# Moving the output-projection products of the first batch's units from the ends of heads two and four to other heads, in a fused decoder-layer kernel

## The chip, the cores and the metric

The kernel runs on one core of one Trainium2 chip. The metric is the device time of one execution in microseconds (us). TensorE is called PE here, VectorE DVE, ScalarE ACT, GpSimd POOL, and SyncE, which issues the DMAs, SP.

## The reference, cut to what matters

```python
x = layernorm(x + attn(x, Wq, Wk, Wv, Wo))          # x: 4 x 512 x 512, 32 query heads, 8 key/value heads
x = layernorm(x + smooth_quant_mlp(x, fside, ctx))  # int8-style MLP, per-batch weights
x = layernorm(x + ffn(x, sign(up), sign(down)))     # 512 -> 2048 -> 512, relu

def attn(x):
    q, k, v = x @ Wq.T, x @ Wk.T, x @ Wv.T          # head width 64, rope on q and k
    p = softmax(causal(q @ k.T / 8))                # 4 query heads share one k/v head
    return (p @ v) @ Wo.T                           # the last product: "output products" below
```

## The kernel before, in words

**Units and heads.** Attention is cut into 32 units. A step g (0 to 15) is one key/value head for two of the four batches; within it b = 0 and b = 1 are the two batches, and unit u = 2g + b. Steps 0 to 7 do batches 0 and 1, steps 8 to 15 batches 2 and 3. A unit has four query heads, h = 0 to 3; the text calls them first to fourth head. In steps 8 to 15 (`half == 1`) single instructions of the quantized MLP of finished batches are slotted in by a written-out schedule (`later(...)`), and after attention the feed-forward part runs.

**One head.** Each engine has a program order of its own, and the engines meet only at semaphores. On PE a head is: transpose blocks 0 and 1 of its probabilities into `ps_t` (L1897), the first two score tiles of the head after it (L1852, into `ps_s`), a *middle* place where one output product may stand, transpose block 2, the last two score tiles, an *end* place for other work, and `values` (L1909, eight matmuls into `ps_o`). DVE meanwhile takes the low parts `pT_lo` (L1562), adds the two halves of the head's result (L1499), makes the row maxima of the next head's scores (`softmax_max`, L1491, four per head), then does the additions to `y` and the reciprocals of the row sums (L1582). ACT exponentiates the next head's four tiles (L1268) and copies the high parts `pT_hi` (L1276). The transposes of a head wait for all four exponentials of that head.

**The end places of a unit.** First head: product "odd" of the next queries (12 matmuls) and `recips` (four transposes, L1919). Second: "vT" (four small transposes, L1865), whose result ACT and DVE take (`low_v`, L1481). Third: "kv" (12 matmuls) and `recips`. Fourth: "even" (12 matmuls).

**Output products.** A unit's result is multiplied by Wo in four products (one per 128 rows), `project_out`, six matmuls each (L1852, `m<-woT_hi,o_hi` and so on). Each is written into the one PSUM tile `m1`, and DVE adds it to `y` in `add_y` (L1514). The `recips` transposes use `m1` too; `normalize` (L1505) reads those. So seven writers of `m1` in a unit of b = 0 and five in one of b = 1 follow one another, in the order of the list `M1_ORDER`; each waits until DVE has read the one before:

```python
def project_out(idx, u, buf, i):
    pe.wait_ge(m1_read, idx - 1)
```

A unit of b = 0 has five products: "out3" of the unit two back (first head, middle), then "out0", "out1", "out2" of the unit before it (second, third and fourth head, middle) and "out3 early" (fourth head, end, behind "even"). A unit of b = 1 has three: "out0" at the end of the second head behind "vT", "out1" and "out2" in the middles of the third and fourth. The unit g = 0, b = 0 has none; so 15 units of b = 0 have five each. In step 15 there is no "kv" and no "even", and in its b = 0 unit four transposes of `y` (L2013) stand ahead of the second, third and fourth of the heads' first transposes; they wait for `low_v` and then for DVE's `lo` parts (L1783). `o_lo` (L1094, on POOL) is what "out0" waits for besides `m1`.

Of the kernel before, what the change touches and what calls it, by code (L numbers as in the profile page):

```python
# [496 lines left out]
def build(nc, x, x_t, wq_t, wkv_t, wo_t, fside, fside_t, ctx, ctx_t, ffn_t, up_s, down_s, out_s, cos_t, sin_t, sin_k_t, out):  # L497
    with ExitStack() as es:
# [186 lines left out]
        def wait(eng, s, v):  # L685

            if not isinstance(v, int) or v > 0:
# [7 lines left out]
        M0_ORDER = [["odd", "vT", "kv", "even"]] * HALF  # L695


        M1_ORDER = [["out3", "recip1", "out0", "out1", "recip0", "out2", "out3 early"],
                    ["recip1", "out0", "out1", "recip0", "out2"]]

        def place(order, b, what):
# [5 lines left out]
        def m1_fill(g, b, what):  # L707
# [3 lines left out]

            return g * sum(len(w) for w in M1_ORDER) + (place(M1_ORDER, b, what) - (len(M1_ORDER[0]) - 1))

# [6 lines left out]
        def before(g, b):  # L720

            return (g, b - 1) if b > 0 else (g - 1, HALF - 1)

        U = STEPS * HALF

# [738 lines left out]
        def _(dve):  # L1464
# [14 lines left out]
            def low_v(u, buf):  # L1479
                dve.wait_ge(v_hi, (u + 1) * 2)  # L1480
                dve.tensor_tensor(v_st[:, buf, :, HD:2 * HD], m0[:, 0:KT * HD].rearrange("p (k d) -> p k d", k=KT),  # L1481
                                  f32(v_st[:, buf, :, 0:HD]), ALU.subtract).then_inc(m0_read, 1)
# [24 lines left out]
            def add_y(g, b, half, what):  # L1507

                to = batch(g, b, half, 2 if what == "out3" else 1)
                if b == 1 and (is_step(g, 0) or is_step(g, HKV)):  # L1510
                    dve.wait_ge(x_in[to], 16 if to == 0 else 32)
                dve.wait_ge(m1_full, m1_fill(g, b, what))
                t = to * QT + int(what[3])
                dve.tensor_tensor(y[:, t, :], y[:, t, :], m1[:, :], ALU.add).then_inc(m1_read, 1)  # L1514
# [32 lines left out]
            def body(g, half):  # L1547
                first = is_step(g, 0)
                last = is_step(g, STEPS - 1)
                for b in range(HALF):  # L1550
                    u = g * HALF + b
                    nxt = not (last and b == HALF - 1)
                    nxt2 = not last
                    prev = not (first and b == 0)
                    for h in range(G):
                        n = u * G + h
                        more = nxt or h < G - 1
                        for k in range(3):
                            dve.wait_ge(p_hi, n * 3 + (k + 1))
                            w = len(T_BLOCKS[k])  # L1560
                            d = slice(PT_FIRST[k], PT_FIRST[k] + w)
                            dve.tensor_tensor(pT_lo[:, d, :], ps_t[:, (h + k) % 2, 0:P * w].rearrange("p (w c) -> p w c", c=P),  # L1562
                                              f32(pT_hi[:, d, :]), ALU.subtract).then_inc(p_lo, 1)
                            if k == 0 and more:
                                softmax_max(n + 1, (h + 1) % 2, 0)
                                softmax_max(n + 1, (h + 1) % 2, 1)
                            if k == 0 and (prev or h > 0):
                                add_o(n - 1, (h - 1) % G, u * 2 + (h - 1) // 2)
                        if more:
                            softmax_max(n + 1, (h + 1) % 2, 2)  # L1570
                            softmax_max(n + 1, (h + 1) % 2, 3)
                        if (is_step(g, 0) or is_step(g, HKV)) and (b, h) == (HALF - 1, G - 1):
                            dve.wait_ge(x_in[half * HALF + HALF - 1], 32)
                        if h == 0 and b != 1 and prev:
                            add_y(g, b, half, "out3")
                        if h > 0 and prev:
                            add_y(g, b, half, f"out{h - 1}")

                        dve.wait_ge(exped, n * 4 + 4)
                        if h % 2 == 0:  # L1580
                            wait(dve, r_repd, u * 2 + h // 2)
                        dve.reciprocal(r_inv[:, :, h // 2, h % 2], row_sum[:, h % 2, :]).then_inc(r_done, 1)  # L1582
                        if half == 1:
                            later("dve1", slot(g, b, h))
                        if h == 0:
                            if prev:
                                normalize(*before(g, b), 1)
                            if nxt:
                                rope_q(m0_fill(g, b, "odd"), u + 1, "odd")
                        if h == 1 and nxt:  # L1590
                            low_v(u + 1, (b + 1) % 2)
                        if h == 2:
                            normalize(g, b, 0)
                        if h == 3:
                            if nxt2:
                                rope_q(m0_fill(g, b, "even"), u + 2, "even")
                            if b == 0 and prev:
                                add_y(g, b, half, "out3 early")
                        if half == 1:
                            later("dve2", slot(g, b, h))  # L1600

# [246 lines left out]
        def _(pe):  # L1848
# [102 lines left out]
            def body(g, half):  # L1951
                first = is_step(g, 0)
                last = is_step(g, STEPS - 1)
                for b in range(HALF):
                    u = g * HALF + b
                    nxt = not (last and b == HALF - 1)
                    nxt2 = not last
                    prev = not (first and b == 0)
                    for h in range(G):
                        n = u * G + h  # L1960
                        more = nxt or h < G - 1
                        ahead = (n + 1, u, h + 1, b % 2) if h < G - 1 else (n + 1, u + 1, 0, (b + 1) % 2)
                        if half == 1:
                            later("pe1", slot(g, b, h))
                        transpose_probs(n, h, 0)
                        transpose_probs(n, h, 1)
                        if more:
                            scores(*ahead, 0)
                            scores(*ahead, 1)
                        if h == 0 and b != 1 and prev:  # L1970
                            project_out(m1_fill(g, b, "out3"), u - 2, b % 2, 3)
                        if h > 0 and prev and (b, h) != (1, 1):
                            project_out(m1_fill(g, b, f"out{h - 1}"), u - 1, (b + 1) % 2, h - 1)
                        if half == 1:
                            later("pe2", slot(g, b, h))
                        transpose_probs(n, h, 2)
                        if more:
                            scores(*ahead, 2)
                            scores(*ahead, 3)
                        if h == 0:  # L1980
                            if nxt:
                                project(m0_fill(g, b, "odd"), (b + 1) % HALF, "odd")
                            if prev:
                                recips(*before(g, b), 1)
                        if h == 1 and nxt:
                            project(m0_fill(g, b, "vT"), (b + 1) % HALF, "vT")
                        if (b, h) == (1, 1):

                            pe.wait_ge(w_lo, w_count(g, "o1"))
                            project_out(m1_fill(g, b, "out0"), u - 1, 0, 0)  # L1990
                        if h == 2:
                            if nxt2:
                                if is_step(g, HKV - 1):
                                    pe.wait_ge(x_lo, KT * (HALF + b + 1))
                                if b == 0:
                                    pe.wait_ge(w_lo, w_count(g + 1, "kv"))
                                project(m0_fill(g, b, "kv"), b, "kv")
                            recips(g, b, 0)
                        if h == 3:
                            if nxt2:  # L2000
                                if b == 0:
                                    pe.wait_ge(w_lo, w_count(g + 1, "q1"))
                                project(m0_fill(g, b, "even"), b, "even")
                            if b == 0 and prev:
                                project_out(m1_fill(g, b, "out3 early"), u - 1, (b + 1) % 2, 3)
                        if half == 1:
                            later("pe3", slot(g, b, h))
                        values(n, h, b % 2)
# [207 lines left out]
```

## Time and profile before

| what | value |
|---|---|
| median of 3 runs | 1388.5 us (1386.83 to 1388.78) |
| the profiled execution: its own time | 1389.54 us |
| its span, first to last instruction | 1387.5 us |
| mean granted TensorE clock | 0.984 of full speed |
| PE matmul busy | 1294.3 us (93% of the span) |
| DVE, ACT, POOL busy | 1012.8, 904.9, 784.7 us (73%, 65%, 57%) |
| attention | up to about 1106 us |

A row of the timeline is: start in us from the span's start, duration, engine, line, operation, output<-inputs, sizes and count; in brackets the idle time of the engine ahead of it and what ended that. Matmuls are pipelined: one of 128x512 is shown with about 0.4 us, but the next starts 0.23 us after it. So PE's cost is read from start to start.

### The profile page before, as it was taken

The numbers are of one execution on the slowest core, as the hardware profiler recorded it, in microseconds if no ns is written. First come the engines' busy times: TensorE is split into PE (matmuls) and PEld (weight loads), VectorE is DVE, ScalarE is ACT, GpSimd is POOL, SyncE is SP. The second block draws the span as 40 slices with busy tenths as digits, with TensorE's granted clock in tenths as the row PEclk, the third lists the DMA queues.
The fourth block names the chain that finished last, engine by engine and source line by source line (L and its number), as shares of the span: only waits on it lengthen the run. The fifth ranks groups of instructions, "written<-read, shape, count | busy, mean of one in ns | idle before, by whom it ended". The sixth has DMA issues, their size and how long they took to land.

```text
span 1387.5 us, 25190 instructions
## 1 busy us (share of the span) xinstructions
PE 1294.3 (93%) x7112; PEld 1075.5 (78%) x7112; DVE 1012.8 (73%) x2492; ACT 904.9 (65%) x2140; POOL 784.7 (57%) x685
## 2 busy tenths in 40 slices
PE   5899999999999999989999999999998899999996
PEld 3788878888888877878877787888776676778784
DVE  3677777777677777898987888778896798875422
ACT  3676777777766776766775776677766756565332
POOL 4555565655556575646873557486661264746553
PEclk8999999999999999999999999999999999999998
DMA  4722222222222223233222222222223602100000
GB/s 138 234 62 54 61 58 63 61 69 62 73 67 54 61 55 92 85 91 85 69 69 54 69 69 55 85 54 69 58 59 121 240 15 71 56 16 31 1 31 30
DMA packets 55285, 98.78 MB, mean 71 GB/s; under 512 B 11792, under 2 KB 13840, under 8 KB 54288
## 3 DMA queue, kind: packets, MB, share of 16 engines
q1 hardware_dynamic: 55184, 97.57, 25.3%
q8 instruction: 47, 0.77, 0.2%
q14 instruction: 54, 0.44, 0.1%
HBM read 51.39 MB, written 4.19 MB: 40 GB/s over the span
## 4 chain that ended last, share of the span: by engine, by line
PE 75%; DVE 10%; ACT 6%; issue 5%; POOL 2%; SPq 0%; DMA 0%; ACTq 0%; DVEq 0%; POOLq 0%
PE m L1852 30%; PE ps_s L1852 9%; PE ps_o L1909 9%; PE ps_t L1897 7%; PE m L2144 7%; PE ps_t L2160 3%; PE ps_s L2160 3%; DVE pT_lo L1562 2%; PE m L1919 2%; ACT pT_hi L1276 2%; DVE o_sum L1505 1%; ACT probs L1268 1%; DVE probs L1491 1%; POOL o_lo L1094 1%; PE pc L2013 1%
## 5 line engine op out<-in xcount | busy, mean ns | idle before, releaser
L1268 ACT ACTIVATE probs<-probs,neg_max 128x128 f32<-128x128 f32 (+3 forms) x512 | 285.3, 559 | 155.7 <-DVE neg_max L1491 155.1
L1562 DVE TENSOR_TENSOR pT_lo<-ps_t,pT_hi 128x512 fp32r<-128x512 f32 (+1 forms) x384 | 220.9, 595 | 141.2 <-ACT pT_hi L1276 138.8
L1491 DVE CUSTOM_DVE_ANT_0 probs<-ps_s,mask 128x128 f32<-128x128 f32 (+3 forms) x512 | 228.3, 482 | 9.4 <-PE ps_s L1852 9.3
L1852 PE MATMUL ps_s<-k_st,q_st 128*128 128x256 f32 (+2 forms) x1024 | 231.7, 348 | 2.4 <-DMA q_st<-q_tmp 2.0
L1897 PE MATMUL ps_t<-ident,probs 128*128 128x128 f32 x1280 | 185.6, 276 | 45.5 <-DVE pT_lo L1562 35.4
L1897 PEld LDWEIGHTS ps_t<-ident,probs 128*128 128x128 f32 x1280 | 147.5, 141 | 70.3 <-DVE pT_lo L1562 44.7
L1276 ACT ACTIVATE pT_hi<-ps_t 128x512 fp32r<-128x512 f32 (+1 forms) x384 | 186.3, 519 | 13.9 <-PE ps_t L1897 10.9
L1094 POOL TENSOR_TENSOR o_lo<-o_sum,o_hi 128x512 fp32r<-128x512 f32 x64 | 81.9, 1279 | 194.1 <-ACT o_hi L1290 194.0
L1909 PE MATMUL ps_o<-pT_hi,v_st 128*128 128x256 f32 (+2 forms) x512 | 169.5, 342 | 0.0
L1909 PE MATMUL ps_o<-pT_lo,v_st 128*128 128x256 f32 (+2 forms) x512 | 156.6, 327 | 0.0
L1852 PEld LDWEIGHTS ps_s<-k_st,q_st 128*128 128x128 f32 x1024 | 151.8, 191 | 5.5 <-issue 2.6
L1144 POOL TENSOR_TENSOR hid_lo<-hid,hid_hi 128x512 fp32r<-128x512 f32 x64 | 84.2, 1315 | 124.4 <-ACT hid_hi L1455 124.4
L1283 ACT ACTIVATE o_part<-ps_o 64x512 f32<-64x512 f32 x128 | 75.9, 593 | 90.6 <-PE ps_o L1909 87.8
L1453 ACT ACTIVATE hid<-m,up_col 128x512 f32<-128x512 f32 x64 | 44.0, 688 | 112.1 <-PE m L2144 109.8
L1852 PE MATMUL m<-woT_hi,o_hi 128*128 128x512 f32 x256 | 105.3, 411 | 6.6 <-POOL o_lo L1094 4.6
L1852 PE MATMUL m<-xT_hi,wqT_hi 128*128 128x512 f32 x256 | 102.6, 401 | 2.8 <-DVEq L1477 2.0
L1909 PEld LDWEIGHTS ps_o<-pT_hi,v_st 128*128 128x128 f32 x512 | 97.8, 191 | 9.4 <-DVE pT_lo L1562 0.5
L1909 PEld LDWEIGHTS ps_o<-pT_lo,v_st 128*128 128x128 f32 x512 | 98.1, 192 | 7.7
L1852 PE MATMUL m<-xT_lo,wqT_hi 128*128 128x512 f32 x256 | 102.8, 402 | 0.0
L1852 PE MATMUL m<-xT_hi,wqT_lo 128*128 128x512 f32 x256 | 102.3, 399 | 0.0
L1852 PE MATMUL m<-woT_lo,o_hi 128*128 128x512 f32 x256 | 101.6, 397 | 0.0
L1852 PE MATMUL m<-woT_hi,o_lo 128*128 128x512 f32 x256 | 101.6, 397 | 0.0
(259 smaller groups left out, 3069.4 us busy)
## 6 DMA issues: line engine op xcount, KB each, us to landing
q_st<-q_tmp SPq DMA_DIRECT2D x512, 64.0 KB, 2.0
raw<-in_wq_t SPq DMA_DIRECT2D x32, 256.0 KB, 3.0
k_st<-k_st SPq DMA_DIRECT2D x64, 128.0 KB, 2.3
raw<-in_wo_t SPq DMA_DIRECT2D x32, 256.0 KB, 3.0
raw_b<-in_ffn_t SPq DMA_DIRECT2D x10, 512.0 KB, 7.5
raw<-in_wkv_t SPq DMA_DIRECT2D x16, 256.0 KB, 3.6
y<-in_x SPq DMA_DIRECT2D x4, 1024.0 KB, 6.8
w_gu<-in_fside_t SPq DMA_DIRECT2D x4, 1024.0 KB, 7.1
```

The costliest lines, as they stand in the source:

```text
L1094: pool.tensor_tensor(o_lo[:, buf, p, :], o_sum[:, :], f32(o_hi[:, buf, p, :]), ALU.subtract).then_inc(o_los, 1)
L1144: pool.tensor_tensor(hid_lo[:, n % 2, :], hid[:, n % 2, :], f32(hid_hi[:, n % 2, :]), ALU.subtract).then_inc(hid_los, 1)
L1268: act.activation(probs[:, h % 2, SO[i]:SO[i] + SW[i]], probs[:, h % 2, SO[i]:SO[i] + SW[i]], ACT.Exp, bias=neg_max[:, h % 2, i:i + 1], sca ...
L1276: act.activation(pT_hi[:, PT_FIRST[k]:PT_FIRST[k] + w, :], ps_t[:, (h + k) % 2, 0:P * w].rearrange("p (w c) -> p w c", c=P), ACT.Copy).the ...
L1283: act.activation(o_part[a:a + HD, :], ps_o[c:c + HD, :], ACT.Copy).then_inc(o_copied, 1)
L1491: dve.tensor_tensor_reduce(out=probs[:, h % 2, SO[i]:SO[i] + SW[i]], in0=ps_s[:, i % 2, 0:SW[i]], in1=mask[:, L - SW[i]:L], scale=-SCALE, ...
L1562: dve.tensor_tensor(pT_lo[:, d, :], ps_t[:, (h + k) % 2, 0:P * w].rearrange("p (w c) -> p w c", c=P), f32(pT_hi[:, d, :]), ALU.subtract).t ...
L1852: i = pe.matmul(dst, a, c, start=(j == 0), stop=(j == len(terms) - 1))
L1897: i = pe.transpose(ps_t[:, (h + k) % 2, P * c:P * (c + 1)], probs[:, h % 2, at:at + P], ident[:, :])
L1909: i = pe.matmul(ps_o[:, q0:L], v_st[:, buf, kt, v0:v0 + P], pT[:, blocks, :], start=(j == 0 and s == 0), stop=(j == 3 and s == 1))
L2144: i = pe.matmul(m0[:, :], w[:, P * k:P * (k + 1)], x2[:, b % 2, k, :], start=(k == 0 and x2 is xT_hi), stop=(k == KT - 1 and x2 is xT_lo))
L2160: i = pe.matmul(down_bank(t), hd[:, m % 2, P * t:P * (t + 1)], w[:, D:2 * D], start=(h == 0 and hd is hid_hi), stop=(h == HT - 1 and hd is ...
```

## The change

In the units of b = 0, "out1" moves from the middle of the third head to the end of the second (behind "vT"), "out2" from the middle of the fourth to the middle of the third, "out3 early" from the end of the fourth to its middle. The writer order of `m1` and the place of DVE's additions go with them: the addition of "out1" now stands behind `low_v` in the second head. Nothing is added or dropped, and units of b = 1 stay as they are.

```diff
-        M1_ORDER = [["out3", "recip1", "out0", "out1", "recip0", "out2", "out3 early"],
+        M1_ORDER = [["out3", "recip1", "out0", "out1", "out2", "recip0", "out3 early"],
                     ["recip1", "out0", "out1", "recip0", "out2"]]
...
+        def out_at(b, h):
+            return ["out0", "out2", "out3 early"][h - 1] if b == 0 else f"out{h - 1}"
...
@@ DVE's order
                         if h > 0 and prev:
-                            add_y(g, b, half, f"out{h - 1}")
+                            add_y(g, b, half, out_at(b, h))
...
                         if h == 1 and nxt:
                             low_v(u + 1, (b + 1) % 2)
+                        if (b, h) == (0, 1) and prev:
+                            add_y(g, b, half, "out1")
...
                                 rope_q(m0_fill(g, b, "even"), u + 2, "even")
-                            if b == 0 and prev:
-                                add_y(g, b, half, "out3 early")
...
@@ PE's order
                         if h > 0 and prev and (b, h) != (1, 1):
-                            project_out(m1_fill(g, b, f"out{h - 1}"), u - 1, (b + 1) % 2, h - 1)
+                            project_out(m1_fill(g, b, out_at(b, h)), u - 1, (b + 1) % 2, int(out_at(b, h)[3]))
...
                             project(m0_fill(g, b, "vT"), (b + 1) % HALF, "vT")
+                        if (b, h) == (0, 1) and prev:
+                            project_out(m1_fill(g, b, "out1"), u - 1, 1, 1)
...
                                 project(m0_fill(g, b, "even"), b, "even")
-                            if b == 0 and prev:
-                                project_out(m1_fill(g, b, "out3 early"), u - 1, (b + 1) % 2, 3)
```

## Rows read from the trace of the kernel before

**Rows 1.** The page: busy time of each engine, then the chain that ended last.
```profile
PE 1294.3 (93%) x7112; PEld 1075.5 (78%) x7112; DVE 1012.8 (73%) x2492; ACT 904.9 (65%) x2140; POOL 784.7 (57%) x685
...
PE 75%; DVE 10%; ACT 6%; issue 5%; POOL 2%; SPq 0%; DMA 0%; ACTq 0%; DVEq 0%; POOLq 0%
```

**Rows 2.** Waits of PE from 80 to 1048 us: total, times, longest.
```profile
PE ps_t L1897 <- DVE pT_lo L1562: 29.8, 31, 3.7
PE ps_t L1897 <- ACT probs L1268: 8.8, 16, 1.3
```

**Rows 3.** Timeline, all engines, second head of the b = 0 unit of step 6.
```profile
431.87 0.46 PE L1865 MATMUL m<-ident,k_tmp 64*128 64x64 f32 x4
432.25 0.50 PE L1909 MATMUL ps_o<-pT_hi,v_st 128*128 128x512 f32 x1
...
433.13 0.68 DVE L1514 TENSOR_TENSOR y<-y,m 128x512 f32<-128x512 f32 x1
...
433.88 0.19 ACT L1268 ACTIVATION_READ_ACCUMULATOR probs<-probs,neg_max 128x1 f32 x1
...
434.21 1.06 PE L1897 MATMUL ps_t<-ident,probs 128*128 128x128 f32 x8 [0.40 <-ACT probs L1268]
```

**Rows 4.** Timeline of PE, same unit: "out0", then the fourth head's end.
```profile
429.27 0.47 PE L1852 MATMUL m<-woT_hi,o_hi 128*128 128x512 f32 x1 [0.24 <-POOL o_lo L1094]
...
430.74 0.38 PE L1897 MATMUL ps_t<-ident,probs 128*128 128x128 f32 x2
...
449.18 0.39 PE L1852 MATMUL m<-woT_hi,o_hi 128*128 128x512 f32 x1
...
450.54 0.39 PE L1909 MATMUL ps_o<-pT_hi,v_st 128*128 128x512 f32 x1
...
451.81 1.03 PE L1897 MATMUL ps_t<-ident,probs 128*128 128x128 f32 x8
```

**Rows 5.** Timeline, second head in steps 5 and 7, b = 0.
```profile
369.81 0.68 DVE L1514 TENSOR_TENSOR y<-y,m 128x512 f32<-128x512 f32 x1
...
370.79 1.09 PE L1897 MATMUL ps_t<-ident,probs 128*128 128x128 f32 x8 [0.40 <-ACT probs L1268]
...
496.43 0.68 DVE L1514 TENSOR_TENSOR y<-y,m 128x512 f32<-128x512 f32 x1
...
498.43 1.06 PE L1897 MATMUL ps_t<-ident,probs 128*128 128x128 f32 x8 [1.21 <-ACT probs L1268]
```

**Rows 6.** Timeline, b = 0 unit of step 15: second head, then fourth head's end.
```profile
1037.62 0.67 DVE L1514 TENSOR_TENSOR y<-y,m 128x512 f32<-128x512 f32 x1
...
1040.18 0.63 PE L2013 MATMUL m<-ident,y 128*128 128x128 f32 x4 [2.12 <-DVE v_st L1481]
1040.64 1.04 PE L1897 MATMUL ps_t<-ident,probs 128*128 128x128 f32 x8
...
1054.12 0.67 DVE L1514 TENSOR_TENSOR y<-y,m 128x512 f32<-128x512 f32 x1
...
1054.81 0.65 DVE L1783 TENSOR_TENSOR xT_lo<-m,xT_hi 128x512 fp32r<-128x512 f32 x1
1054.85 0.50 PE L1852 MATMUL m<-woT_hi,o_hi 128*128 128x512 f32 x1 [1.85 <-DVE y L1514]
...
1059.64 1.04 PE L1897 MATMUL ps_t<-ident,probs 128*128 128x128 f32 x8
```

**Rows 7.** Timeline of PE: two more waits of about two microseconds.
```profile
1046.84 0.66 PE L1919 MATMUL m<-ident,r_rep 128*128 128x128 f32 x4 [1.81 <-DVE y L1514]
...
1079.49 0.66 PE L1919 MATMUL m<-ident,r_rep 128*128 128x128 f32 x4 [2.39 <-DVE y L1514]
```

**Rows 8.** Stretches behind such waits; the column after the five engines is the granted clock.
```profile
1056.10:1059.60 3.50, 3.50 (x14) 3.20 (x13) 0.69 (x1) 0.57 (x1) 0.00 (x0) 0.52 0.97 394
1079.90:1083.30 3.40, 3.40 (x17) 3.21 (x16) 0.89 (x2) 1.23 (x2) 1.27 (x1) 0.53 1.03 419
1047.00:1050.00 3.00, 3.00 (x25) 2.91 (x25) 1.14 (x2) 1.55 (x4) 1.03 (x1) 1.00 0.60 146
```

## The prediction, made before the changed kernel was run

> **What bounds the kernel.** I read the page first: PE is busy for 93% of the span, and the chain that ended last lies on PE for three quarters of it [rows 1]. So within attention the question is what makes PE idle, not how much another engine has to do. The table of PE's waits then shows two main kinds [rows 2]: transposes that wait for `pT_lo`, and transposes at the start of a head that wait for the exponentials, 16 times and 8.8 us in all. Last I read the timeline of single units. The second head of every b = 0 unit has the shortest end place, "vT" alone, and there the third head's transposes start 0.40 us late, since the last exponential's sum ends at 434.07 [rows 3]. The fourth head has the longest end: "even" and a product, 449.18 to 450.54 [rows 4]. PE's matmuls are the same before and after; the change pays only through waits that go or come.
>
> **Fourth head.** "out3 early" leaves its end. From its first matmul to the first of `values` is 450.54 - 449.18 = 1.36 us [rows 4], all of it on PE's path: -1.36. `values` then ends 1.36 earlier, at about 450.45. The next transposes can start there if the exponentials are ready. The addition of "out2" does not stand in the way, for the product now in the middle of the fourth head takes exactly the place and the size of the one that was there. The same holds for "out2" in the middle of the third. These two trades cost nothing; what covers their reads of `m1` is the same as before ("kv" with `recips`, and the transposes and scores).
>
> **Second head, the new wait.** "out1" stands behind "vT" and ahead of `values`. As every writer of `m1` it waits for the read of the one before, here DVE's addition of "out0". DVE does that only after the fourth row maximum of the next head, and that follows PE's last score tile directly ahead of "vT". So DVE is late by construction: the addition starts at 433.13 and ends at 433.81 [rows 3], while PE is through with "vT" and would go on at 432.25. How long the hand-over takes is seen in step 15, where the same situation exists already (a product with nothing but scores between it and the product before): the addition ends at 1054.12 + 0.67 = 1054.79, the matmul starts at 1054.85 [rows 6], 0.06 us later. So "out1" starts at 433.87, 1.62 us after the point where PE would have gone on. A product that starts from a standing PE takes 430.74 - 429.27 = 1.47 us [rows 4], `values` takes 451.81 - 450.54 = 1.27 [rows 4], and the third head's transposes start at 433.87 + 1.47 + 1.27 = 436.61 instead of 434.21: +2.40. The old 0.40 us wait for the exponentials is in this sum, since they are long done. Net for the unit: 2.40 - 1.36 = +1.04 us.
>
> **What is queued behind the wait.** On PE: "out1", `values`, the next transposes, in order; ACT's copy of `ps_o` waits for `values`. On DVE the new addition stands behind `low_v` and ahead of the scheduled MLP work and the third head's `pT_lo`, but that needs transposes which PE does after "out1" and `values`, 2.7 us later; the 0.6 us of the addition are hidden there. "out2", one head on, needs that addition read: "out1" ends at about 435.3 and its addition at 436.0, while "out2" can start no sooner than 1.4 us of transposes and scores behind 436.6. SP's and POOL's queues get nothing new.
>
> **The other units.** By the same arithmetic on their own rows: in step 5 the addition ends at 370.49, the transposes would start at 370.49 + 0.06 + 2.74 = 373.29 against 370.79 [rows 5], +2.50, net +1.14. Steps 1 to 4 repeat this to within 0.01; steps 8 to 14 repeat step 6 to within 0.01. In step 7 ACT has extra work and PE waited 1.21 us already; there it is 497.11 + 2.80 = 499.91 against 498.43 [rows 5], +1.48, net +0.12. Sum over steps 1 to 14: 5 x 1.14 + 8 x 1.04 + 0.12 = +14.1.
>
> **Step 15** differs. In the second head PE waited 2.12 us for `low_v` before four transposes [rows 6]. Now "out1" starts at 1038.29 + 0.06 = 1038.35, `values` ends at 1041.09, the four transposes take 0.46 (1040.18 to 1040.64), and the head starts at 1041.55 instead of 1040.64: +0.9. In the fourth head the standing wait of 1.85 us, "out3 early" and a slow `values` behind it go away. PE will wait instead for the low part that ends at 1054.81 + 0.65 = 1055.46, then do 0.46 of transposes: 1056.0 against 1059.64 [rows 6], -3.6. Net -2.7. All units together: +11.4 us.
>
> **The granted clock.** The waits here are long enough to ask whether the clock drops from its 2.4 GHz level to the 1.2 GHz one. After PE stood for 1.85 and for 2.39 us [rows 6, 7] the clock fell for about 3.4 us (0.52 and 0.53 [rows 8]); after 2.12 us and 1.81 us [rows 6, 7] the rows go on at full pace, and the stretch behind the second shows 1.00 [rows 8]. So two of the four waits of this size cost a fall. The new waits are 1.6 us long, 14 of them (that of step 15 apart), a little shorter than all four: I take one in three, between four and five falls. A fall costs 3.5 x (1 - 0.52) = 1.7 us where PE sets the pace. That is +7.5 us; the bounds are no fall (0) and two in three (+16). The Trainium skill, "TensorE: Matmul & The Clock Gate", section "Why this matters for your kernels", advises to avoid PE-idle gaps between bursts of matmuls, and the gap that it names is longer than all four waits here. By that page the clock would stay up and the sum would be +11.4; this trace's fall after 1.85 us speaks against it.
>
> **Sum.** The profiled execution took 1389.54 us, 1.04 above the median of the runs (1388.5), and 2.04 more than its span; I count the difference of +11.4 + 7.5 = +18.9 from the median: 1407.4 us.
>
> **Rivals.**
>
> *A: the wait, with the clock up.* 1388.5 + 11.4 = 1399.9. For it: every new wait is shorter than the shortest one that was followed by a fall. One fall would still belong here. Chance 0.30.
>
> *B: the clock falls in most of the units.* 1388.5 + 11.4 + 16 = 1415.9. For it: "vT" and the transposes beside the wait are small work, and half of the comparable waits cost a fall. Chance 0.15.
>
> *C, on the other side: the addition of "out0" is not late.* If DVE were done with it by the time "vT" is, "out1" would follow without a wait: third head at 432.25 + 1.37 + 1.27 = 434.89, +0.68, net -0.68 a unit; 14 of them -9.5, with step 15's fourth head -3.6, about 1375.5. It decides at a wait of about 0.7 us, above which a unit loses. Against it: the fourth row maximum alone ends after 433.1 [rows 3], and it can't start before the scores that precede "vT". Chance 0.05.
>
> *D: the added time is taken out of later waits.* The 29.8 us of waits for `pT_lo` [rows 2] would have to shrink by what the second heads add. They hang on ACT's and DVE's order behind `values`, which moves along with PE; only single ones, where DVE's MLP work is late in the third head, can be absorbed. If it happened in steps 8 to 14: about 1388.5 + 5.7 + 1.0 + 0.1 - 2.7 = 1392.6 or, with some large waits gone, no change. Chance 0.08 (half of it within 0.2% of before or faster).
>
> **The numbers.** My forecast, the wait and some falls of the clock (2 to 7), has the remaining 0.42: 1407.4, its own range 1402 to 1412. The 8-in-10 range reaches down to just below A and up to B: 1397 to 1417. About 0.2% (2.8 us) is what a measurement of this kernel can tell from no change. Slower by more: forecast, A, B and half of D, 0.91; same 0.03; faster 0.06.
>
> **What would show it.** In the new profile, a wait of about 1.5 us ahead of a `m<-woT_hi,o_hi` matmul, released by DVE's `y` at L1514's successor, in all 15 b = 0 units, right behind "vT"; no wait for exponentials at their third heads; the fourth head's end 1.36 us shorter; in step 15 the 1.85 us wait gone; stretches of clock near 0.5 behind some of the new waits, and the mean clock below 0.984. I am wrong if DVE's addition is found ahead of "vT"'s end, if the waits for `pT_lo` shrink by as much, or if the clock does something else.

## The result, and the profile of the changed kernel

The changed kernel takes 1398.9 us (median of 5 runs, 1395.3 to 1401.1), the kernel before 1388.5 us (5 runs, 1386.8 to 1390.7): a ratio of 1.0074, 95% interval 1.0062 to 1.0086. That is 10.4 us slower, against 18.9 forecast; the time lies in the wide range of the prediction (1397 to 1417), and below the forecast's own 1402 to 1412. The profiled execution took 1398.74 us with a span of 1397.0 us.

First the page of the changed kernel; its row that begins with PE's busy time answers to the first of [rows 1], its last row to the second. Most lines of the program now have numbers higher by five (L1514 is L1519).

```profile
span 1397.0 us, 25180 instructions
...
PE 1290.2 (92%) x7112; PEld 1074.9 (77%) x7112; DVE 1010.5 (72%) x2492; ACT 905.9 (65%) x2140; POOL 784.9 (56%) x685
...
PE 71%; DVE 12%; issue 7%; ACT 5%; POOL 4%; SPq 0%; DMA 0%; DVEq 0%; POOLq 0%; ACTq 0%
```

PE has the same work and a lower share; DVE's share of the chain went up, from 10% to 12%, PE's went down, from 75% to 71%. Next PE's waits, from 80 to 1058 us:

```profile
PE ps_t L1902 <- DVE pT_lo L1567: 28.2, 30, 3.6
PE m L1857 <- DVE y L1519: 24.1, 15, 1.9
...
PE ps_t L1902 <- ACT probs L1273: 1.7, 2, 1.3
```

A kind of wait is new: an output product for DVE's addition to `y`, 15 times, 24.1 us. The waits for the exponentials went from 16 and 8.8 us to 2 and 1.7 us, those for `pT_lo` hardly moved (29.8 before [rows 2]). Now the timeline of the second head in step 6, all engines, which answers to [rows 3]:

```profile
435.32 0.46 PE L1870 MATMUL m<-ident,k_tmp 64*128 64x64 f32 x4
...
436.61 0.68 DVE L1519 TENSOR_TENSOR y<-y,m 128x512 f32<-128x512 f32 x1
...
437.34 0.50 PE L1857 MATMUL m<-woT_hi,o_hi 128*128 128x512 f32 x1 [1.56 <-DVE y L1519]
...
438.84 0.39 PE L1914 MATMUL ps_o<-pT_hi,v_st 128*128 128x512 f32 x1
...
440.12 1.03 PE L1902 MATMUL ps_t<-ident,probs 128*128 128x128 f32 x8
```

From "vT" to the next head's transposes it is now 4.80 us, before 2.34: +2.46, where 2.40 was forecast. The addition ends at 437.29, the matmul starts 0.05 us later.

The starts of `values` in the 128 heads, changed kernel minus kernel before, give the whole account. Taken is the second of its eight matmuls, since the first is drawn out by 0.1 us where it stands right behind "vT". Each number below is that shift in us at the first to the fourth head of a unit:

```
step 1  b=0    -2.06   1.06   0.42  -0.94        step 9  b=0     5.30   9.07   9.28   7.93
step 2  b=0    -0.95   2.15   1.49   0.14        step 10 b=0     8.16  11.03  10.18   8.84
step 5  b=0     2.36   5.46   4.81   3.45        step 12 b=0    10.11  13.13  11.63  10.28
step 6  b=0     3.47   6.48   5.85   4.50        step 12 b=1    10.39   6.36   6.79   6.78
step 6  b=1     4.52   4.51   4.52   4.52        step 13 b=0     6.78  11.56  10.70   9.33
step 7  b=0     4.52   7.41   5.55   4.23        step 15 b=0    11.87  15.48  14.35  10.54
step 8  b=0     4.24   7.24   6.62   5.29        step 15 b=1    10.76  10.79  10.69   9.63
```

How to read it: within a unit the shift jumps up in the second head, gives back 0.65 in the third and 1.35 in the fourth; in a unit of b = 1 it stands still. Steps 1 to 5 add 1.10 us each, steps 6 and 8 about 1.05, step 7 takes 0.29 off. From the first head of step 1 to the last of step 15 the changed kernel loses 11.7 us. It had come 2.06 us early to step 1: that is in the lead-in, which the change doesn't touch, and where the clock was granted differently (0.94 over the first 80 us, 0.91 before). The last experiment below keeps the old order and shows 0.94 there too, so the change isn't what makes it.

### The profile page after: what moved, and what is told of

It reads as the page before. It is cut to its first block, busy times and chain, and to the rows that moved or that the text cites. A ratio compares the mean times of both kernels' runs of the same rounds, so it can differ in the third digit from the quotient of the medians.

```text
span 1397.0 us, 25180 instructions
## 1 busy us (share of the span) xinstructions
PE 1290.2 (92%) x7112; PEld 1074.9 (77%) x7112; DVE 1010.5 (72%) x2492; ACT 905.9 (65%) x2140; POOL 784.9 (56%) x685
## 4 chain that ended last, share of the span: by engine, by line
PE 71%; DVE 12%; issue 7%; ACT 5%; POOL 4%; SPq 0%; DMA 0%; DVEq 0%; POOLq 0%; ACTq 0%
PE m L1857 28%; PE ps_s L1857 9%; PE ps_o L1914 9%; PE m L2149 7%; PE ps_t L1902 7%; PE ps_t L2165 3%; PE ps_s L2165 3%; DVE pT_lo L1567 2%; PE m L1924 2%; DVE probs L1496 2%; ACT pT_hi L1281 2%; POOL o_lo L1099 1%; DVE o_sum L1510 1%; DVE y L1519 1%; ACT o_hi L1295 1%
## 5 line engine op out<-in xcount | busy, mean ns | idle before, releaser
L1857 PE MATMUL m<-woT_hi,o_hi 128*128 128x512 f32 x256 | 107.3, 419 | 28.9 <-DVE y L1519 24.1
```

Of the source, the lines that this page charges most:

```text
L1857: i = pe.matmul(dst, a, c, start=(j == 0), stop=(j == len(terms) - 1))
```

## The experiments

All are the changed kernel with the edit shown, except where the text says otherwise. Times are medians; the kernel before took 1387.9 to 1388.7 us beside them.

### The addition of "out0" earlier in DVE's order

```diff
                             if k == 0 and (prev or h > 0):
                                 add_o(n - 1, (h - 1) % G, u * 2 + (h - 1) // 2)
+                            if k == 1 and (b, h) == (0, 1) and prev:
+                                add_y(g, b, half, "out0")
...
-                        if h > 0 and prev:
+                        if h > 0 and prev and (b, h) != (0, 1):
                             add_y(g, b, half, out_at(b, h))
```

> The changed kernel, with DVE's addition of out0 in the second head of b = 0 placed ahead of the third pT_lo instead of behind the four row maxima. Theory (the late addition is the whole loss): out1 follows vT without a wait, each unit gains 0.7 us on the kernel before and step 15 some 3.6 us, so about 1375.5 us, against 1398.9 for the changed kernel and 1388.5 before. The addition pushes the maxima and exponentials 0.4 to 0.6 us later, to about 434.6 in the unit of step 6, still ahead of the 434.9 at which PE comes to the transposes. Rival (the second head gets too full whatever the order, since DVE and ACT are pushed back too): 1390 to 1399 us, with a wait for pT_lo or the exponentials in place of the one for y.

Measured: 1370.9 us, ratio to before 0.9874 (0.9858 to 0.9891). The theory holds, and the version beats both kernels, by 17 and by 28 us. It lies 4.6 us below the expected 1375.5: steps 1 to 6 gain 0.6 us each on the kernel before, as rival C of the prediction had it (0.68), and most of the rest is a gain of 4 us in step 12 that is told further down. Its timeline in step 6, all engines:

```profile
425.82 0.67 DVE L1519 TENSOR_TENSOR y<-y,m 128x512 f32<-128x512 f32 x1
...
426.29 0.46 PE L1872 MATMUL m<-ident,k_tmp 64*128 64x64 f32 x4
...
426.68 0.50 PE L1859 MATMUL m<-woT_hi,o_hi 128*128 128x512 f32 x1
...
428.57 0.19 ACT L1273 ACTIVATION_READ_ACCUMULATOR probs<-probs,neg_max 128x1 f32 x1
...
429.45 1.03 PE L1904 MATMUL ps_t<-ident,probs 128*128 128x128 f32 x8
```

The addition is over at 426.49, and "out1" follows "vT" with no idle time. From "vT" to the transposes it is 3.16 us. The exponentials are done at 428.76, before PE comes to them.

### The same addition a little later

The edit is the same with `k == 2` in place of `k == 1`.

> As the one before, but the addition of out0 behind the third pT_lo and ahead of the last two row maxima, 0.6 us later. Theory: out1 waits about 0.55 to 0.65 us for it; a unit comes out 0.0 to 0.1 us better than before and step 15 gains 3.6 us, so 1383 to 1385 us. Rival (a wait of this length is covered by something else): 1376, as with no wait; rival (second head too full): 1390 to 1399.

Measured: 1381.1 us, ratio 0.9947 (0.9931 to 0.9964), 2 us below the expected range. PE's waits for `y` are 8.4 us in all, 16 times.

### The addition later still

```diff
                         if (b, h) == (0, 1) and prev:
+                            add_y(g, b, half, "out0")
                             add_y(g, b, half, "out1")
```

(with the `!= (0, 1)` line of the first experiment)

> The changed kernel with the addition of out0 made still later, behind low_v. Theory: out1 starts about 1.9 us later than in the changed kernel (wait of 3.5 us instead of 1.6), 15 times, +28 us: 1427 us, if the clock falls no more often than before. If each wait of 3.5 us is followed by a fall of the granted clock that costs 1.7 us and nothing else goes away: another 20 to 25 us, about 1450. Rival (the wait is not what PE's time hangs on): 1399.

Measured: 1449.8 us, ratio 1.0441 (1.0424 to 1.0459). PE's waits for `y`, and the stretches of 84 to 500 and 500 to 1100 us, whose clock stands after the five engines:

```profile
PE m L1858 <- DVE y L1519: 53.9, 15, 4.7
...
84.00:500.00 416.00, 384.06 (x2159) 328.74 (x2158) 281.65 (x771) 276.63 (x718) 218.97 (x188) 0.98 0.24 59
500.00:1100.00 600.00, 543.43 (x3060) 460.62 (x3058) 465.94 (x1199) 396.48 (x1005) 355.05 (x311) 0.96 0.25 66
```

The waits grew by 29.8 us, the time by 50.9. The rest goes with the clock: in the changed kernel the same two stretches show 1.00 and 0.98. Each of the 15 waits (3.3 to 4.7 us) has a fall of the clock with it, which begins during the wait or up to 1.3 us behind it. That of step 2, where the wait ends at 184.29:

```profile
184.50:187.90 3.40, 3.40 (x9) 2.63 (x9) 0.69 (x1) 0.00 (x0) 1.18 (x2) 0.50 0.44 101
```

That is the case for which 1450 us was expected. So the price of a wait has two parts, its own length and, where it is long, a slower TensorE behind it.

The time rises with the wait over the four places of one addition. Waits of PE for `y` in an `m<-woT_hi,o_hi` matmul against the time:

| addition of "out0" | waits, us | time, us |
|---|---|---|
| behind the second `pT_lo` | 0.8 | 1370.9 |
| behind the third `pT_lo` | 8.4 | 1381.1 |
| behind the maxima (the changed kernel) | 24.1 | 1398.9 |
| behind `low_v` | 53.9 | 1449.8 |

### "out1" behind `values`

```diff
-                        if (b, h) == (0, 1) and prev:
-                            project_out(m1_fill(g, b, "out1"), u - 1, 1, 1)
...
                         values(n, h, b % 2)
+                        if (b, h) == (0, 1) and prev:
+                            project_out(m1_fill(g, b, "out1"), u - 1, 1, 1)
```

> The changed kernel with out1 behind the second head's values on PE instead of ahead of them; DVE's order as in the changed kernel. Theory: 1.27 of the 1.62 us of the wait is covered by values; the third head's transposes start 1.1 us later than before the change, the fourth head gains 1.36, so a unit gains 0.2 us and step 15 about 3.6: about 1381.5 us. Rival (the product's own 1.47 us behind vT is what costs, wherever it stands in the second head's end): about 1398.

Measured: 1378.7 us, ratio 0.9931 (0.9915 to 0.9948). DVE's order is that of the changed kernel and the product is still in the second head; only PE has something to do while DVE finishes. The waits for `y` are 2.3 us in all, and the time is 2.8 us below the expected 1381.5. So the product's own 1.47 us were never the loss.

### The wait filled with matmuls of no use

```diff
                         if (b, h) == (0, 1) and prev:
+                            wait(pe, o_added, n)
+                            for j in range(6):
+                                pe.matmul(ps_o[:, :], o_hi[:, 1, 0, 0:P], woT_hi[:, 0, :], start=True, stop=True)
                             project_out(m1_fill(g, b, "out1"), u - 1, 1, 1)
```

> The changed kernel with six matmuls of no use on PE ahead of out1 in the second heads of b = 0, written into the ps_o tile that values overwrites; they take 1.4 of the 1.6 us for which PE stands there. Nothing else changes, so without a part of the clock the time is that of the changed kernel, 1399. If the low-clock stretches behind four of the new waits cost what I had counted (1.6 to 1.7 us each) and nothing takes their place: 1392. If falls of the clock come elsewhere instead: 1398 to 1400.

Measured: 1391.7 us (10 runs, 1390.4 to 1397.1), ratio 1.0034 (1.0017 to 1.0051), close to the 1392 expected if the new falls go. The median is 7.2 us below the changed kernel's, the ratios (1.0034 and 1.0074) put the difference at 5.6 us, with six matmuls more in each of 15 units. The slowest of the 10 runs had a lower mean clock than the profiled one (0.987 against 0.991). Its timeline of PE in step 6:

```profile
434.31 0.46 PE L1870 MATMUL m<-ident,k_tmp 64*128 64x64 f32 x4
434.70 1.65 PE L1995 MATMUL ps_o<-woT_hi,o_hi 128*128 128x512 f32 x6
436.33 0.50 PE L1857 MATMUL m<-woT_hi,o_hi 128*128 128x512 f32 x1
...
439.11 1.03 PE L1902 MATMUL ps_t<-ident,probs 128*128 128x128 f32 x8
```

"vT" to transposes is 4.80 us, as in the changed kernel. In steps 1 to 8 the two kernels keep their distance to 0.15 us. They part in steps 9, 13, 14 and 15, by 1.56, 1.50, 1.57 and 1.56 us, and by 1.1 in step 10. In the changed kernel the four second heads of those steps are followed by a slow stretch:

```profile
637.80:641.20 3.40, 3.40 (x11) 2.78 (x12) 2.07 (x3) 0.56 (x3) 3.40 (x5) 0.60 0.50 113
914.80:918.20 3.40, 3.09 (x7) 2.48 (x8) 0.90 (x4) 1.54 (x5) 3.40 (x5) 0.52 0.46 104
983.00:986.40 3.40, 3.40 (x10) 2.67 (x10) 1.82 (x4) 0.49 (x2) 3.40 (x4) 0.53 0.48 110
1050.60:1054.00 3.40, 3.40 (x13) 2.94 (x12) 1.97 (x3) 1.27 (x3) 1.42 (x2) 0.63 0.43 97
437.50:440.50 3.00, 3.00 (x18) 2.65 (x19) 1.11 (x2) 0.76 (x4) 3.00 (x4) 1.00 0.48 109
```

The last line is the one of step 6, where the clock stayed up behind a wait of 1.56 us; the first stands behind one of 1.55. So the same wait can cost 1.6 us more or nothing. With PE kept busy these four falls are gone, 6.2 us in the profiled executions. The 1.1 us of step 10 are not one of them: there a fall of 6.8 us behind a wait of 3.2 us for `pT_lo`, which the kernel before has too, came out half as long.

### "out3 early" at the fourth head's end again

```diff
-                        if h > 0 and prev and (b, h) != (1, 1):
+                        if h > 0 and prev and (b, h) not in ((1, 1), (0, 3)):
                             project_out(m1_fill(g, b, out_at(b, h)), u - 1, (b + 1) % 2, int(out_at(b, h)[3]))
...
                                 project(m0_fill(g, b, "even"), b, "even")
+                            if b == 0 and prev:
+                                project_out(m1_fill(g, b, "out3 early"), u - 1, 1, 3)
```

(and DVE's addition of it behind `rope_q` again)

> The changed kernel with out3 early at the end of the fourth head again, behind even, and so with nothing in the fourth head's middle. My step says that a product's place within the fourth head is free of charge. Against it stands the pattern of heads with an empty middle, where PE waits 0.7 us for pT_lo: then 15 times 0.7 us, about 1409 us. If the places are equal: 1399.

Measured: 1418.2 us, ratio 1.0213 (1.0177 to 1.0249), 19 us more than the changed kernel, where I had 10 for the wait. PE's waits for `pT_lo` over 80 to 1150 us rose from 32 times and 29.8 us in the changed kernel to:

```profile
PE ps_t L1904 <- DVE pT_lo L1567: 42.6, 46, 3.7
```

Fourteen waits more; those of the fourth heads in steps 1 to 7 are 0.75 to 0.85 us long. Such a fourth head costs 1.0 us more in all, 0.2 above its wait. Of the rest 2.4 us are in the b = 1 unit of step 12 (below), 2 us stood already before step 1 (the clock of the first 80 us is 0.91 here), and the clock fell more often (0.982 against 0.985 as the mean). So here a place in the middle is worth more than one at the end.

### The change in step 15 alone

The kernel before, with the new order and places where `g == STEPS - 1` and the old ones elsewhere:

```diff
-            return g * sum(len(w) for w in M1_ORDER) + (place(M1_ORDER, b, what) - (len(M1_ORDER[0]) - 1))
+            order = M1_ORDER if isinstance(g, int) and g == STEPS - 1 else M1_OLD
+            return g * sum(len(w) for w in order) + (place(order, b, what) - (len(order[0]) - 1))
```

> The kernel before, with the change made in step 15 alone (one unit of b = 0). Theory: the second head loses 0.9 us to the wait for the addition, the fourth gains 3.6 because its standing wait of 1.85 us and the product leave its end; with a fall of the clock behind the new wait, as in the changed kernel, 1.7 of it go again. So 1 to 2.7 us faster than before: 1386 to 1387.5 us. Rival (the loss of 10 us comes from step 15 or from what follows it): slower than before.

Measured: 1386.0 us, ratio 0.9989 (0.9980 to 0.9998). It gains 1 to 2 us, as expected; the interval only just leaves out no change. The new wait, 1.77 us, has a fall of the clock behind it here too.

### The early addition in the old order

The kernel before, with nothing but the first experiment's edit of DVE's order.

> The kernel before, in its old order, with nothing but DVE's addition of out0 in the second head of b = 0 moved ahead of the third pT_lo. Theory (the early addition is good only because out1 follows): nothing waits for it in the old order, and it pushes the row maxima and so the exponentials back by 0.4 us, for which PE already waited 0.40 us in the third head; 14 times 0.4 us, about 1394 us. Rival (the early addition itself is what makes the version with 1370.9 us fast): well under 1388, down to 1375.

Measured: 1391.1 us, ratio 1.0022 (1.0013 to 1.0032). The early addition by itself costs 3 us, where 6 had been expected. PE's wait in the third head of step 6 is longer than the 0.40 us of [rows 3]:

```profile
434.43 1.06 PE L1899 MATMUL ps_t<-ident,probs 128*128 128x128 f32 x8 [0.67 <-ACT probs L1268]
```

So neither half is good alone: the products' new places cost 10 us, the early addition 3 us, and both together save 17.

## Why the prediction was right, and where it was off

**The wait in the second head** was right in mechanism, place, number and size: 15 waits, 24.1 us, of 1.42 to 1.90 us each; forecast were 14 of 1.6 us, and one in step 15 to which the prediction gave no length of its own. The four places of the addition, and the version with the wait covered by `values`, show that it is the cause. Taking it away turns +10.4 us into -17.

**The unit's sum.** Forecast +1.14 in steps 1 to 5 and +1.04 in steps 6 and 8; measured 1.10 and 1.05. Step 7 was to be +0.12 and is -0.29. Step 10 comes to +0.7 and step 12 to +0.3 in its b = 0 unit, both forecast at 1.04. Part of the added time is taken out of a later wait in step 12: the kernel before waited 0.49 us for `pT_lo` at 840.5, in the third head, and the changed one doesn't.

```profile
840.52 0.44 PE L1897 MATMUL ps_t<-ident,probs 128*128 128x128 f32 x2 [0.49 <-DVE pT_lo L1562]
```

That is rival D on a small scale. In steps 7 and 10 it is not shown what takes the 0.4 us each. Steps 9, 11, 13 and 14 add 1.3, 1.3, 1.1 and 0.9 us once the falls of the clock behind their new waits are taken off. Steps 1 to 14 so come to +12.9, forecast +14.1. I had named rival D and given it no share of the sum.

**The fourth head** gave back 1.35 us, forecast 1.36. That the *middle* place costs nothing held because both kernels fill it. Emptied, it costs 1.0 us a head, and the same empty middles stand in the first two heads of every b = 1 unit of both kernels.

**Step 15** was forecast at -2.7 without a fall of the clock and so about -1.0 with one; its b = 0 unit went from +11.87 to +10.76, -1.1, with the fall of 1050.6 us in it. The parts fit as well: +2.5 up to the third head (0.9 and the fall), then -3.6. PE's wait for the low part, at 1069.94, was 1.31 us:

```profile
1069.94 0.63 PE L2018 MATMUL m<-ident,y 128*128 128x128 f32 x4 [1.31 <-DVE xT_lo L1788]
```

**The granted clock** is the step that failed: "between four and five falls ... +7.5 us". The falls behind the new waits were there, four of them, and the filled version puts them at 6.2 us. What I left out is that falls of the kernel before would go, other than the one inside the -3.6 of step 15. The stretch of 500 to 1100 us shows 0.98 in both kernels:

```profile
500.00:1100.00 600.00, 552.55 (x3187) 468.49 (x3187) 484.59 (x1244) 416.30 (x1046) 348.41 (x306) 0.98 0.28 76
```

In attention the kernel before has falls at 595, 729, 868, 1056 and 1080 us, the changed one at 601, 638, 737, 915, 983 and 1051 us; each lasts 3.4 us, those at 729, 868 and 737 us twice that. Three of the old ones are missing in the changed kernel. That behind the 1.85 us wait of step 15 goes with its cause, and it is in the -3.6 that I had counted. That behind the 2.39 us wait [rows 7] is gone although the wait is still there; the last head of step 15 comes 1.1 us less late for it. And the double one of step 12 goes where the wait ahead of it gets shorter, next; that unit of b = 1 gains 3.6 us in all, 1.5 of them the shorter wait, which leaves 2.1 for the clock. So both kernels spend the same time at the low clock, seven times 3.4 us. Counted as the forecast counts, with the fall of 1056 us inside the -3.6, the clock's share is 6.2 - 1.1 - 2.1 = 3.0 us, not 7.5.

**The whole difference** between the profiled executions, +9.5 us against +18.9, is then: 4.5 us less for the clock, 1.5 less for the shorter wait of step 12, 1.3 less in the sum of steps 1 to 14, and 2.1 in the lead-in. The first is the term that the prediction mis-sized, the second nothing in it foresaw, and the last has nothing to do with the change. That the time comes to rival A's 1399.9 is luck: A had said that the clock would not fall behind the new waits, and it fell four times.

**A gain that nothing of mine foresaw** is step 12, b = 1: -4.0 us at its second head. DVE's rows there, in the kernel before:

```profile
864.77 3.27 DVE L1615 TENSOR_TENSOR sm_b<-sm_b,bounds 128x4 f32<-128x4 f32 x1
868.07 0.16 DVE L1616 TENSOR_TENSOR sm_b<-sm_b,bounds 128x4 f32<-128x4 f32 x1
```

and in the changed kernel:

```profile
875.15 0.76 DVE L1620 TENSOR_TENSOR sm_b<-sm_b,bounds 128x4 f32<-128x4 f32 x1
875.94 1.19 DVE L1621 TENSOR_TENSOR sm_b<-sm_b,bounds 128x4 f32<-128x4 f32 x1
```

The two small operations end 1.5 us sooner against what is around them, PE's wait for the `pT_lo` behind them falls from 3.71 to 2.23 us, and the clock, which had fallen for 6.8 us there, stays up. The first row is the kernel before, the second the changed one:

```profile
868.50:875.30 6.80, 6.23 (x18) 4.77 (x19) 4.21 (x13) 5.24 (x15) 2.52 (x2) 0.50 0.22 50
878.00:884.80 6.80, 6.80 (x41) 5.80 (x42) 5.93 (x20) 6.55 (x18) 3.99 (x6) 1.00 0.26 60
```

The same -4.0 appears in the version with the early addition, and it is lost again (+3.0 against the changed kernel) where "out3 early" stands at the fourth head's end. In all ten versions it goes with that edit: the six with "out3 early" in the fourth head's middle show a wait of 2.2 us here, the four with it at the end one of 3.7. Why DVE's start shifts by 0.07 us against POOL's row with it, I did not test.

**What stays open.** Whether a wait of 1.5 to 2.4 us is followed by a fall can't be told from its length alone, and the runs here don't settle what decides. So some us of the difference between any two of these kernels hang on it; the runs of the changed kernel themselves spread over 5.8 us.

## What to carry to other kernels

A move of a product on PE is also a move of its reader: before putting a second writer of one buffer into a stage, look at where in the other engine's program order the read of the first stands, not at how busy that engine is. Here one line in DVE's order turned a loss of 10 us into a gain of 17, and either edit alone lost. And when a change adds waits of some microseconds to TensorE, count the clock's falls on both sides, those that come and those of the old kernel that may go.

## What the runs showed of the hardware

**A wait of 1.5 us can be enough for a fall of the clock, and length alone doesn't decide it.** Behind waits of 1.55 and 1.90 us the clock fell to about half (0.60 and 0.52 above), behind one of 1.56 it stayed at 1.00. Useless matmuls in the gap were worth 5.6 to 7.2 us. The Trainium skill, "TensorE: Matmul & The Clock Gate", section "Why this matters for your kernels", advises against idle gaps longer than all of these; by it none of these falls should have come, and the measurement decides.

**A tiny DVE operation beside a row of POOL operations can take as long as several of them.** The 128x4 operation at 864.77, of a kind that takes 0.16 us (the next one, at 868.07), took 3.27 us while POOL ran without a pause. POOL's rows of that stretch, kernel before:

```profile
863.04 1.29 POOL L1055 TENSOR_TENSOR k_st<-k_tmp,k_st 64x512 fp32r<-64x512 f32 x1 [2.02 <-ACT k_st L1251]
864.30 1.27 POOL L1094 TENSOR_TENSOR o_lo<-o_sum,o_hi 128x512 fp32r<-128x512 f32 x1
865.53 1.25 POOL L1060 TENSOR_TENSOR q_tmp<-q_tmp 128x512 f32<-128x512 f32 x1
866.76 1.25 POOL L1061 TENSOR_TENSOR q_tmp<-q_tmp 128x512 f32<-128x512 f32 x1
```

It ended at 868.04, just behind POOL's last at 868.01, and passed two seams between POOL's operations (865.5, 866.8) without getting in. In the changed kernel, 0.07 us later against POOL's row, it ended at 875.91, beside the first seam:

```profile
874.61 1.28 POOL L1099 TENSOR_TENSOR o_lo<-o_sum,o_hi 128x512 fp32r<-128x512 f32 x1
875.85 1.26 POOL L1065 TENSOR_TENSOR q_tmp<-q_tmp 128x512 f32<-128x512 f32 x1
```

The Trainium skill, "SBUF — State Buffer", section "SBUF: two separate sides", describes the pair of ports that DVE and GpSimd share as an exclusive lock, held for a whole instruction. The trace agrees on the kind of delay; that the waiting engine gets its turn when that one instruction ends, it shows in the one case and not in the other.
